# 64x64 tiles for scores and outputs, and the last two experts summed on chip, in a vision block with eight experts

## What is computed

```python
h = conv_patches(x) + pos_table[ids]                  # (16, 49, 192)
# attention on layernorm(h), 12 heads of 64, causal
scores = einsum(q, k) / 8; softmax; z = pattern @ v; h = h + z @ W_O + b_O
# experts on layernorm(h), flattened to 784 tokens, E = 8, the two largest of softmax(logits)
buf = x of the tokens that chose expert e, at most cap = 245 rows an expert
z = rmsnorm(2 * buf) * norm_w;  g, u = z @ w13.T      # hidden 512
y = buf + (silu(g) * u) @ w2.T
out = h + sum over the two choices of share * y       # dropped rows count zero
```

## Time and profile before

| | us |
|---|---|
| median of 3 runs | 227.73 (226.76 to 228.80) |
| profiled execution, its own time | 228.95 |
| span of the profiled execution | 227.1 |
| PE, PEld busy | 187.7, 169.1 |
| DVE, ACT, POOL busy | 132.7, 107.8, 81.5 |
| mean granted TensorE clock | 0.934 |

### The profile page before, as it was taken

The page is one execution under the profiler, slowest core; times in us unless marked ns, Lnnn a source line. Parts: engine busy times, 40 slices in busy tenths (PEclk is TensorE's granted clock), DMA queues, the critical chain, the costliest instruction groups (busy, mean ns, idle before and its releaser), DMA issues.

```text
span 227.1 us, 4181 instructions
## 1 busy us (share of the span) xinstructions
PE 187.7 (83%) x1503; PEld 169.1 (74%) x1506; DVE 132.7 (58%) x388; ACT 107.8 (47%) x223; POOL 81.5 (36%) x126
## 2 busy tenths in 40 slices
PE   6796999979899997979598856699999999997000
PEld 1794998968899987869497632499999999996000
DVE  6258747776777168698766772637457645720014
ACT  2043673246446655746638940437656765632000
POOL 9323002233532305284663785000522442245400
PEclk9999999999999999999859999589999999999555
DMA  6983790180030000010010111583468867230273
GB/s 179 398 328 103 264 298 40 20 348 9 0 118 25 27 0 4 13 45 16 28 40 0 42 49 45 177 316 128 149 202 286 277 171 241 78 104 23 50 203 117
DMA packets 10774, 28.16 MB, mean 124 GB/s; under 512 B 3182, under 2 KB 5323, under 8 KB 9568
## 3 DMA queue, kind: packets, MB, share of 16 engines
q1 hardware_dynamic: 7312, 24.32, 32.5%
q0 software_dynamic: 2816, 2.60, 4.3%
q10 hardware_dynamic: 624, 0.97, 1.4%
HBM read 24.08 MB, written 6.75 MB: 136 GB/s over the span
## 4 chain that ended last, share of the span: by engine, by line
PE 50%; issue 12%; DVE 12%; POOL 9%; DMA 9%; ACT 6%; POOLq 0%; SPq 0%; ACTq 0%; DVEq 0%
PE ps L530 9%; PE ps L303 5%; POOL slots L794 4%; PE ps L517 3%; PE ps L518 3%; PE ps L514 3%; PE ps L513 3%; PE ps L519 3%; DMA xp<-patches 2%; DMA parts<-qT,toke 2%; PE ps L391 2%; POOL sm L786 2%; ACT probT L586 2%; DMA kB<-parts 2%; DVE gap L918 2%
## 5 line engine op out<-in xcount | busy, mean ns | idle before, releaser
L820 POOL DMA_INDIRECT parts<-qT,toke x16 | 22.7, 1416 | 49.9 <-ACT qT L710 47.7
L1052 DVE TENSOR_TENSOR v<-v,ps 128x246 f32<-128x246 f32 x32 | 12.5, 407 | 21.1 <-ACT v L701 21.1
L978 DVE TENSOR_TENSOR wqkv<-raw,wqkv 128x1024 fp32r<-128x1024 f32 x16 | 19.5, 1222 | 7.5 <-DMA slots<-row,slot 4.2
L794 POOL DMA_INDIRECT slots<-row,slot x16 | 17.1, 1071 | 17.7 <-DVE slot L964 11.3
L303 PE MATMUL ps<-convw,xp 128*98 128x192 f32 x96 | 19.9, 368 | 2.7 <-DMA xp<-patches 1.9
L530 PE MATMUL ps<-xp,v 128*123 128x192 f32 x128 | 22.0, 326 | 0.0
L303 PEld LDWEIGHTS ps<-convw,xp 128*98 128x98 f32 x96 | 17.5, 189 | 4.7 <-DMA xp<-patches 2.8
L786 POOL TENSOR_TENSOR sm<-sm,smax 128x588 f32<-128x588 f32 x8 | 10.6, 1330 | 28.5 <-DVE smax L882 28.2
L530 PEld LDWEIGHTS ps<-xp,v 128*123 128x123 f32 x128 | 20.6, 186 | 0.0
L513 PE MATMUL ps<-zeA,wqkv 128*128 128x246 f32 x64 | 19.1, 298 | 0.0
L701 ACT ACTIVATE v<-ps 128x246 f32<-128x246 f32 x32 | 12.0, 375 | 14.8 <-PE ps L519 13.5
(11 more groups left out here) (148 smaller groups left out, 510.3 us busy)
## 6 DMA issues: line engine op xcount, KB each, us to landing
raw<-w SPq DMA_DIRECT2D x8, 1025.0 KB, 6.9
xp<-w SPq DMA_DIRECT2D x8, 384.0 KB
xp<-patches SPq DMA_DIRECT2D x8, 294.0 KB, 5.5
raw<-w_qkv SPq DMA_DIRECT2D x3, 768.0 KB, 9.4
slots<-blank SPq DMA_DIRECT2D x8, 196.0 KB, 3.9
xp<-slots SPq DMA_DIRECT2D x8, 196.0 KB
parts<-zeros SPq DMA_DIRECT2D x1, 1176.0 KB, 8.2
bases<-base SPq DMA_DIRECT2D x8, 73.5 KB
```

Of the source, the lines that this page charges most:

```text
L794: P.indirect_dma_start(slots, bass.IndirectOffsetOnAxis(slot[:, p % PH, k:k + 1], 0), row[:, p % 2, k, :], None, bounds_check=EXPERTS * ST ...
L820: P.indirect_dma_start(parts, bass.IndirectOffsetOnAxis(toke[:, e, r:r + 1], 0), ye[0:EROWS, e % 2, r, :], None, bounds_check=TOPK * N + E ...
L978: last = V.tensor_tensor(wsp[:, j, 1, half, :], raw13[j][:, half * W13:(half + 1) * W13], wsp[:, j, 0, half, :].bitcast(f32), ALU.subtract)
```

## The change

1. Scores use tiles of 64 rows by 64 columns: for each image and head one matmul of 64 rows and 49 columns (24 a pair of images, 12 before). The keys lie densely in `kT`, written by DVE alone, 128 partitions at a time; `kB`, its memset and ScalarE's key copies go.
2. Outputs likewise: 24 matmuls of 64 rows (one image) and 49 columns. `probT` is dense, and `diagonal` is one copy of 128x588. The layout of `zs` is kept by the two copies that write it.
3. `base` stays on chip for all pairs (98 partitions x 8 x 192); `bases` and its nine DMAs go. Results are now laid out as token-of-pair by pair.
4. Experts 6 and 7 don't go through `parts`. Each slot row also carries its token's number. For each of their four halves DVE builds a 123x784 matrix of ones and zeros (`member`), ScalarE and DVE make the weighed output as high and low halves (`yo`), and PE adds all rows to their tokens in banks 0 to 3 (`combine`, 16 matmuls a half).
5. PE's order at the end is `down(5)`, `down(6)`, `gate_up(7)`, `combine(0)`, `combine(1)`, `down(7)`, `combine(2)`, `combine(3)`.
6. SP alone reads `parts` back, in four reads of rows of 768 bytes, as soon as expert 5's sends have landed. DVE adds these (98x768, four additions), then PSUM's four quarters, and SP stores each quarter.

```diff
@@ scores
-                        last = mm(ps[SLOT * i:SLOT * (i + 1), hp // 3, (hp % 3) * PT:(hp % 3 + 1) * PT], qT[:, hp, p % PH, i, :],
-                                  kB[:, hp, p % PH, i].rearrange("p a t -> p (a t)"), start=True, stop=True)
+                        c = (hp % 3) * PT + i * TOK
+                        for a in range(2):
+                            r = slice(DH * a, DH * (a + 1))
+                            last = mm(ps[r, hp // 3, c:c + TOK], qT[r, hp, p % PH, i, :], kT[r, hp, p % PH, i, :], start=True, stop=True)
@@ outputs
-                    for a in range(2):
-                        hd = 2 * hp + a
-                        last = mm(ps[DH * a:DH * (a + 1), 4 + hp // 3, (hp % 3) * PT:(hp % 3 + 1) * PT],
-                                  v[:, p % PH, DH * hd:DH * (hd + 1)], probT[:, hd].rearrange("p i t -> p (i t)"), start=True, stop=True)
+                    for i in range(2):
+                        r = slice(SLOT * i, SLOT * (i + 1))
+                        for a in range(2):
+                            hd = 2 * hp + a
+                            last = mm(ps[DH * a:DH * (a + 1), 4 + i, hp * TOK:(hp + 1) * TOK], v[r, p % PH, DH * hd:DH * (hd + 1)], probT[r, hp, a, :],
+                                      start=True, stop=True)
@@ diagonal
+                A(probT[:].rearrange("k (b h) a t -> k b (h a) t", b=2), ps[:, 2:4, 0:384].rearrange("k b (h q) -> k b h q", q=SLOT)[:, :, :, 0:TOK],
+                  ACT.Copy).then_inc(pt_ready, 1)
@@ PE, the end
+            def combine(i):
+
+                pe.wait_ge(member_ready, i + 1)
+                pe.wait_ge(yolo_ready, i + 1)
...
+                for p in range(PAIRS):
+                    o = ps[0:PT, p // 2, (p % 2) * D:(p % 2 + 1) * D]
+                    mm(o, member[:, i, p * PT:(p + 1) * PT], yo[:, i, 0, :], start=(i == 0 and p % 2 == 0), stop=False)
+                    last = mm(o, member[:, i, p * PT:(p + 1) * PT], yo[:, i, 1, :], start=False, stop=(i == len(ONCHIP) - 1 and p % 2 == 1))
...
+            down(EXPERTS - 2)
+            gate_up(EXPERTS - 1)
+            for i in range(2):
+                combine(i)
+            down(EXPERTS - 1)
+            for i in range(2, len(ONCHIP)):
+                combine(i)
@@ SP, the end
+            all_sent(sp)
+            for b in range(PARTS):
+                for k in range(TOPK):
+                    load_part(sp, k, b)
+            for b in range(QUARTERS):
+                sp.wait_ge(out_ready, b + 1)
+                sp.dma_start(quarter(out, b), quarter_of(base, b)).then_inc(stored, 16)
@@ DVE, the end
+            for i in range(len(ONCHIP)):
+                members(i)
+            for i in range(2):
+                weigh_lo(i)
+            for jt in range(JT):
+                gated(EXPERTS - 1, jt)
+            for i in range(2, len(ONCHIP)):
+                weigh_lo(i)
+            n4 = PAIRS // PARTS
+            for b in range(PARTS):
+                for k in range(TOPK):
+                    dve.wait_ge(ld_part[k][b], 16)
+                    added = mark(V.tensor_tensor(base[:, n4 * b:n4 * (b + 1), :], base[:, n4 * b:n4 * (b + 1), :], part[:, k, n4 * b:n4 * (b + 1), :], ALU.add))
+                    dve.wait_ge(dve_seq, added)
+            for b in range(QUARTERS):
+                dve.wait_ge(combined, b + 1)
+                V.tensor_tensor(quarter_of(base, b), quarter_of(base, b), ps[0:PT, b, 0:2 * D].rearrange("q (p d) -> q p d", p=2), ALU.add).then_inc(out_ready, 1)
```

More of the change, by code:

```diff
@@ L51, with vit_block @@
 IGNORE = -100000.0
-def vit_block(nc, patches, conv_w, w_qkv, w_o, w13, w2, by_column, by_row, before, blank, zeros, out):
+def vit_block(nc, patches, conv_w, w_qkv, w_o, w13, w2, by_column, by_row, before, blank, zeros, numbers, out):
     f32, f32r, bf16, u32 = mybir.dt.float32, mybir.dt.float32r, mybir.dt.bfloat16, mybir.dt.uint32
@@ L216, in embedded, with quarter, quarter_of, all_sent @@
             return (s + PH + 2,) if -2 <= s < 2 else ()
+        def quarter(t, b):
+            n = PAIRS // QUARTERS
+            return t[b * n * PT:(b + 1) * n * PT, :].rearrange("(p q) d -> q p d", q=PT)
+        def quarter_of(t, b):
+            n = PAIRS // QUARTERS
+            return t[:, b * n:(b + 1) * n, :]
+        def all_sent(engine):
+            for j in range(2):
+                for r in range(2):
+                    engine.wait_ge(sent[j][r], 16 * (EXPERTS // 2 - 1))
+        def load_part(engine, k, b):
+            n = PAIRS // PARTS
+            rows_ = parts[k * N + b * n * PT:k * N + (b + 1) * n * PT, :]
+            engine.dma_start(part[:, k, b * n:(b + 1) * n, :], rows_.rearrange("(p q) d -> q p d", q=PT)).then_inc(ld_part[k][b], 16)
         @block.sync
@@ L253, in _ @@
                 load_w2(j, j)
-            for p in range(PAIRS):
-                sp.wait_ge(base_ready, p + 1)
-                sp.dma_start(bases[p * PT:(p + 1) * PT, :], base[:, p % 2, :]).then_inc(based[p % 2], 16)
+            sp.dma_start(tokens_row[:], numbers).then_inc(ld_numbers, 16)
             for a in range(2):
@@ L716, in _ @@
                 silu(0, jt)
-            for e in range(EXPERTS):
-                if e + 1 < EXPERTS:
-                    for jt in range(JT):
-                        silu(e + 1, jt)
-                        if e + 2 < EXPERTS and jt < 2:
-                            split_hi(e + 2, jt)
-                if e + 2 < EXPERTS:
-                    x_hi(e + 2)
-                weigh(e)
-            for j in range(2):
-                for r in range(2):
-                    act.wait_ge(sent[j][r], 16 * EXPERTS // 2)
-            for b, (lo, hi) in enumerate(HALVES):
-                act.dma_start(part[:, 1, lo:hi], parts[N:2 * N, :].rearrange("(q n) d -> q (n d)", q=LAID)[:, lo:hi]).then_inc(ld_part[1][b], 16)
+            for e in range(EXPERTS - 2):
+                for jt in range(JT):
+                    silu(e + 1, jt)
+                    if jt < 2:
+                        split_hi(e + 2, jt)
+                x_hi(e + 2)
+                weigh(e)
+            weigh(EXPERTS - 2)
+            for jt in range(JT):
+                silu(EXPERTS - 1, jt)
+            weigh(EXPERTS - 1)
         @block.gpsimd
@@ L1058, in _, with members, weigh_lo @@
                 split_lo(1, half)
+            def members(i):
+                e, r = ONCHIP[i]
+                V.tensor_scalar(member[:, i, :], tokens_row[:], xe[0:EROWS, e % 2, r, D + 2:D + 3], None, ALU.is_equal).then_inc(member_ready, 1)
+            def weigh_lo(i):
+                e, r = ONCHIP[i]
+                dve.wait_ge(yohi_ready, i + 1)
+                V.scalar_tensor_tensor(yo[:, i, 1, :], ps[0:EROWS, 6 + r, 0:D], cwe[:, e, r:r + 1], yo[:, i, 0, :].bitcast(f32),
+                                       ALU.mult, ALU.subtract).then_inc(yolo_ready, 1)
             for e in range(2):
@@ L1124 @@
         "zeros": np.zeros((LAID, TOPK * N * D // LAID), np.float32),
+        "numbers": np.broadcast_to(np.arange(N, dtype=np.float32), (EROWS, N)),
     }
```

137 lines of the change are left out of this document (58 added, 79 removed).

## The result

The changed kernel took 217.6 us (median of 4 runs, 215.58 to 220.35) where the kernel before took 227.25 (median of 4, beside it on the same chip): a ratio of 0.954, 95% interval 0.942 to 0.966, so faster, and by more than forecast (221.7; that is 5.5 us, against the 9.7 found). Over the 49 runs of the kernel before that stand beside the experiments the mean is 225.6, over the ten of the changed kernel 217.9. So the change is worth 7 to 10 us; how much of that it owes to its own edits is what the experiments ask.

The account below looks back on a forecast made before the run. PE was taken to bound attention's first half and the experts, DVE and ACT its second half, the read-back chain the tail. Diagonal -2.35, tiles +1.8, tail -5.5 sum to -6.05: 221.7 us from a median of 227.73, range 217.0 to 227.0.

Parts of the forecast that it names:

- the tail: End of kernel: on-chip sums for experts 6 and 7 and an earlier read-back end the span at 221.6, not 227.1: -5.5 us.
- Rival A: Tail: the read-back of `parts` comes late, 2.6 us worse, total 224.3 us; chance 0.15.
- PE is not last: Tail: PE's 64 combine matmuls cost 5.8 us where PE had been idle, and DVE ends last.
- the term of outputs: Attention outputs in 64x64 tiles: 28 ns a pair with two tiles loading together, a block of 1.57 us.
- d: Change in time of one block of scores or outputs from 64x64 tiles, against 1.23 us before; taken as +0.3 us.
- the lower bound: Attention tiles: all time scales with columns streamed, an outputs block 0.75 us (-0.5), a scores block 1.23 us (0).
- the +1.8: Attention tiles: six blocks on PE's path (outputs 0, 1, 2, 6, scores 3, 4) get slower, +1.8 us in all.
- the -2.35: Attention, one diagonal copy for four: PE's waits shrink by 0.95, 0.39 and 1.0 us in steps 0, 1 and 3.
- it counts only where PE waits: Attention: the diagonal copy's 1.0 us shorter latency gains only in steps where PE waits for it, there counted as gain.
- the attention part: Attention: the diagonal's -2.35 us and the tiles' +1.8 us, together a gain of 0.55 us.
- case D: Attention: tiling pays fully, or the stretch at a clock of 0.57 goes; total 217.9 to 219.9 us; chance 0.18.
- the sign of being wrong: Prediction wrong if a block exceeds 2.2 us, the clock falls elsewhere, or late small-row stores take well over 3 us.

Follow-up runs that it names:

- e2: The change without its attention part (old tiles, four diagonal copies, memsets), against the kernel before: 217.17 us, ratio 0.971.
- e10: The changed kernel with only the last expert summed on chip, PE running down(6), gate_up(7), down(7), then two combines: 216.65 us, ratio 0.957 to the kernel before.
- e11: The changed kernel with gate_up(7) ahead of down(6) and all combines behind down(7): 213.43 us, ratio 0.944 to the kernel before.
- e6: The changed kernel with the diagonal copied in four instructions again: 217.25 us, ratio 0.961 to the kernel before.
- e15: The changed kernel with the old order of last products, no softmax row maximum, and the diagonal copied in four: 210.90 us, ratio 0.941 to the kernel before.
- e3: The changed kernel with memsets of `part` and `kT` put back ahead of DVE's work: 216.04 us, ratio 0.968 to the kernel before.
- e4: The changed kernel again, unchanged, on another chip: 218.07 us, ratio 0.972 to the kernel before.
- e8: The kernel before with dummy matmuls in PE's idle places of steps 4 to 7 and more ahead of the experts: 223.89 us, ratio 0.993.
- e9: The changed kernel with one of DVE's four part additions given to POOL: 216.28 us, ratio 0.955 to the kernel before.
- after: The changed kernel in its first measurement and profile, against the kernel before: 217.6 us, ratio 0.954.
- e1: The kernel before with the change's attention part alone (64x64 tiles, one diagonal copy, keys by DVE): 222.75 us, ratio 0.989.
- e13: The changed kernel with the old order of the last products, run again as a base: 215.78 us, ratio 0.957 to the kernel before.
- e14: The changed kernel with the old order of last products and no softmax row maximum or its subtraction: 209.30 us, ratio 0.936 to the kernel before.
- e12: The changed kernel with the old order of last products and one part addition on POOL: 214.32 us, ratio 0.946 to the kernel before.

## Why the prediction was right and wrong

*Sign and mechanism of the tail: right.* Forecast -5.5; the tail part alone (e2) and the changed kernel have 63.0 to 63.3 us from the first `down` to the end, against 69.1 to 69.3: about -6. Step by step, from the first `down`: additions start at 54.6 by the forecast, 54.5 measured; the four last 3.9 (3.8), and the end comes at 63.3 (63.5). PE ends 6.7 us before the span does (forecast about 7). Rival A (a late read-back) did not happen, and no wait for `part` stands in the tail.

*What I read past in it.* "PE is not last: its 64 combine matmuls cost 5.8 us where PE had been idle" is wrong for half of them: 32 stand ahead of `down(7)` and so ahead of the last weighing, and all but 0.9 us of their time falls where PE wasn't idle (e10). The sum had them in its times, so it came out right; but the remark hid that the new order gives away 2.8 us there (e11), 1.7 by the combines and 1.1 by the place of `down(6)`.

*Tiles: the term of outputs was mis-sized.* I took two tiles side by side for both blocks: right for scores (28 ns forecast, 29 measured), wrong for outputs, where four do: 15 ns, a block of 0.92 us instead of 1.57, d = -0.3 instead of +0.3. This lies near what I had called the lower bound (0.75). Four of the six blocks that I charged are outputs: 4 x 0.65 = 2.6 us less than the +1.8, so -0.8 (scores, at 1.60, were as forecast).

*Diagonal: the -2.35 were not there.* I took PE's waits for `probT` out of the path. They did go, but PE then waits for `zs`, `both` and `h2T` (3 us more of these), since the chain in steps 0 to 3 passes mostly to the softmax of DVE, POOL and ACT, which the copy is no part of. e6 and e15 put it at 0 to 1 us (0.1 at one clock, in e15). The step that failed is "it counts only where PE waits": a wait that ends is worth only what the next late thing leaves. The two errors point opposite ways, and it is luck that the attention part came near its forecast: -0.55, against about -1 by stage lengths (e3, e4, e8, e9 and after) and -2.5 with an interval from -5.1 to +0.2 by e1's ratio.

*The clock: counted as a rival, was part of the result.* The sum put it at no change. The profile of before held a stretch at 0.57, and I named its going as case D with 0.18; the sign of being wrong that I gave, a clock that falls in another place, is what came. The stretch went in the first measurement and came back in e4. The entry of the experts was a term at nothing, and gave 1.9 us in the first profiles by the clock alone. The start, no term either, gave 1.7 by PE's pace from 9 to 13 us, which differs between profiles of like kernels too (e3, e4). The first comparison's 9.7 us are about 6 of the tail, and 3.7 of attention, start and entry, which vary from run to run; the pooled difference is 7.7. I can't split the rest to the end: about 1 us is the attention part's, and e8 shows 1.7 to be had by fillers alone. That the tighter attention makes low stretches rarer would fit and was not shown; e1, with the tiles, has low slices.

*The range* ended at 217.0, 0.2 above the ratio's centre times the median of before (0.954 x 227.3 = 216.8), since I let tail and clock come out well only one at a time.

*What would have been better.* The change without its new order (e11, e13: mean 214.4), and beyond it the softmax without its maximum (209.3), which is the same function as long as the exponential of the scores doesn't overflow.

## What to carry to other kernels

A wait of the busiest engine is not a gain to be counted in full: walk on from it to the next thing that comes late, and price the removal by the difference. When work is given to an engine with idle time at its end, look which side of its last needed product the work is queued on; here 32 matmuls, 2.9 us of work, cost 1.7 us ahead of it (they also filled a wait) and nothing behind it. When both totals scatter by 2%, compare stage lengths between fixed landmarks, and ask of each stage whether its clock was the same.

## What the runs showed of the hardware

Pairs of weight load and matmul in 64x64 f32 tiles follow each other at 47 ns in one tile, 29 in two and 15 in four tiles used in turn, with tiles of different row halves side by side, which in scores write the same bank. The Trainium skill, "TensorEngine Tiling (Array Packing)", Instruction Overhead, has a fixed cost of about 60 cycles for each matmul. By that page an estimate is 25 ns at 2.4 GHz; 15 ns a pair is below that, so it is at least not a spacing. The Trainium skill, "TensorEngine Tiling (Array Packing)", Gotcha 1, says that different row tiles cannot use one bank at the same time. It did not show in the time: a pair in scores, with two tiles and one bank, takes twice what it takes in outputs, with four tiles and a bank for each row half.

POOL holds DVE up. A DVE subtraction of two numbers a row takes 0.14 to 0.16 us six times and 1.71 and 1.75 us twice, each time while POOL has two operations in a row (timelines of the changed kernel, DVE and POOL):

```profile
89.19 0.14 DVE L945 TENSOR_TENSOR gap<-top 98x1 f32<-98x1 f32 x1
96.70 1.71 DVE L945 TENSOR_TENSOR gap<-top 98x1 f32<-98x1 f32 x1
...
96.65 0.60 POOL L807 TENSOR_TENSOR h<-h,rowwise 98x192 f32<-98x192 f32 x1
97.20 1.18 POOL L812 TENSOR_TENSOR sm<-sm,smax 128x588 f32<-128x588 f32 x1
```

It ends at 98.41, POOL's second at 98.38. In e14, where POOL has no L812, all eight take 0.14 to 0.16. So part of what the maximum cost was this, 3.2 us in two steps on the chain of DVE; it was not measured apart from the maximum itself. The Trainium skill, "SBUF — State Buffer", SBUF: two separate sides, tells of a port pair that DVE, with two inputs in SBUF, and GpSimd hold by turns for a whole instruction; this trace agrees (1.71 us for 0.14). POOL's addition of 98x768 took 1.82 us in e9, where it starts 1.8 us ahead of DVE's additions, and 2.10 in e12, where it starts within one of them; DVE's own take 0.97 either way. That POOL waits for DVE too would fit and was not shown.
